# A decoder layer on one core: another order of the steps in the cross-attention loop

## What is computed

```python
x = _layernorm(x + _L0_attn_ref(x, W_K, W_Q, W_V, W_O))
# cross-attention; IMG_LEN = 257 > 256, so only the image half has tokens
q = rms_norm(linear(x, q_w, q_b), norm_q_w).reshape(B, L, NH, HD)      # NH 16, HD 16
k_img = rms_norm(linear(ctx_img, k_img_w, k_img_b), norm_k_img_w).reshape(B, -1, NH, HD)
v_img = linear(ctx_img, v_img_w, v_img_b).reshape(B, -1, NH, HD)
x = _layernorm(x + linear(attention(q, k_img, v_img), o_w, o_b))
x = _layernorm(x + _L0_ffn_ref(x, gate_w, gate_b, w1, b1, w2, b2))     # top 2 of 8 experts
```

## Time and profile before

| | us |
|---|---|
| median of 3 runs | 660.62 |
| lowest and highest | 660.0 and 664.72 |
| the profiled execution, whole | 664.72 |
| its span, first to last instruction | 663.0 |
| PE busy in the span | 559.1 |
| DVE, ACT, POOL busy | 364.5, 308.3, 166.1 |

### The profile page before, as it was taken

How to read it: one execution, slowest core, us unless ns; L and a number is a source line. 1 busy time by engine, 2 the same in 40 slices (tenths; PEclk the granted TensorE clock), 3 DMA queues, 4 the chain that set the end, 5 groups by cost and what they waited for, 6 DMA issues and landing times.

```text
span 663.0 us, 12586 instructions
## 1 busy us (share of the span) xinstructions
PE 559.1 (84%) x3867; PEld 482.7 (73%) x3867; DVE 364.5 (55%) x1134; ACT 308.3 (46%) x831; POOL 166.1 (25%) x267
## 2 busy tenths in 40 slices
PE   3899999999999999999686898783627999999940
PEld 2789898989989898988564555452416999999940
DVE  5175656565555656566755467621253655655645
ACT  1464545545554545445442565432123546446423
POOL 4131313131211122010368850105230000000153
PEclk9999999999999999999887799868567999999985
DMA  8640403123040405500000000001211442552324
GB/s 276 210 175 17 175 17 136 54 76 113 22 152 32 158 0 223 236 1 1 1 0 1 1 4 2 1 1 64 72 55 31 160 165 76 220 198 91 120 80 123
DMA packets 18403, 58.74 MB, mean 89 GB/s; under 512 B 3169, under 2 KB 7521, under 8 KB 13761
## 3 DMA queue, kind: packets, MB, share of 16 engines
q1 hardware_dynamic: 14048, 38.00, 16.0%
q10 hardware_dynamic: 1728, 12.58, 5.0%
q0 software_dynamic: 2592, 7.74, 3.4%
HBM read 35.83 MB, written 22.41 MB: 88 GB/s over the span
## 4 chain that ended last, share of the span: by engine, by line
PE 71%; DVE 8%; POOL 7%; issue 5%; ACT 3%; DMA 3%; DVEq 1%; POOLq 0%; SPq 0%; ACTq 0%
PE bank L549 12%; PE bank L551 11%; PE bank L550 11%; PE bank L927 6%; PE bank L606 4%; PE bank L588 4%; PE bank L596 3%; PE bank L763 3%; PE bank L779 3%; PE bank L607 2%; PE bank L587 2%; DVE w_lo L1516 2%; PE bank L707 2%; POOL x_slots L468 1%; PE bank L810 1%
## 5 line engine op out<-in xcount | busy, mean ns | idle before, releaser
L1151 ACT ACTIVATE hT<-bank,b 128x128 f32<-128x128 f32 x152 | 53.4, 368 | 57.6 <-PE bank L927 55.1
L927 PE MATMUL bank<-xgT,w 128*128 128x128 f32 x608 | 73.4, 280 | 1.2 <-DVE xgT L1509 0.7
L927 PEld LDWEIGHTS bank<-xgT,w 128*128 128x128 f32 x608 | 71.7, 196 | 1.8 <-issue 1.1
L1047 ACT ACTIVATE xPT<-bank 128x512 f32<-128x512 f32 x64 | 38.1, 599 | 61.8 <-PE bank L763 61.1
L1315 DVE TENSOR_REDUCE xnmax<-bank 128x2 f32<-128x512 f32 x64 | 43.8, 690 | 40.6 <-PE bank L742 39.9
L549 PE MATMUL bank<-xT_hi,wqk_hi 128*128 128x512 f32 x128 | 56.3, 440 | 11.0 <-DVE wqk_lo L1191 11.0
L1200 DVE CUSTOM_DVE_ANT_0 Sm<-bank,mask 128x128 f32<-128x128 f32 (+1 forms) x128 | 40.7, 356 | 33.7 <-PE bank L588 33.7
L967 ACT ACTIVATE Pr<-Sm,nmax 128x128 f32<-128x128 f32 x64 | 25.8, 403 | 70.5 <-DVE nmax L1200 70.4
L551 PE MATMUL bank<-xT_hi,wqk_lo 128*128 128x512 f32 x128 | 51.0, 399 | 0.0
L550 PE MATMUL bank<-xT_lo,wqk_hi 128*128 128x512 f32 x128 | 50.9, 398 | 0.0
L549 PE MATMUL bank<-w_hi,hT_hi 128*128 128x256 f32 x152 | 44.7, 294 | 3.9 <-DVE hT_lo L1537 3.9
(11 more groups left out here) (213 smaller groups left out, 1514.0 us busy)
## 6 DMA issues: line engine op xcount, KB each, us to landing
w<-in_w ACTq DMA_DIRECT2D x12, 1024.0 KB, 6.3
w_raw<-in_w_attn SPq DMA_DIRECT2D x32, 256.0 KB, 3.5
x_slots<-w SPq DMA_DIRECT2D x8, 1024.0 KB, 5.5
y_slots<-w SPq DMA_DIRECT2D x7, 1024.0 KB, 7.4
w<-in_w SPq DMA_DIRECT2D x4, 1024.0 KB, 7.8
xg<-x_slots SPq DMA_DIRECT2D x20, 128.0 KB
y_slots<-ys POOLq DMA_DIRECT2D x19, 128.0 KB, 2.0
xT_raw<-in_xT SPq DMA_DIRECT2D x2, 512.0 KB, 5.6
```

The lines of the kernel that those rows point to most:

```text
L927: last = mm(bank[f % 4][:, 0:P], w1e[:, c, f * P:(f + 1) * P], xgT[:, c, :], start=c == 0, stop=c == DC - 1)
L1047: A(xPT[j % 8][:, :, :], ps_xt[j % 2][:, :].rearrange("p (a n) -> p a n", a=2), ACT.Exp)\
L1151: A(hT[:, f, :], bank[f % 4][:, 0:P], ACT.Gelu_apprx_tanh, bias=b1[:, e, f:f + 1])\
```

## The change

All three lists of steps are rearranged; no operation is added or left out. PE now issues `x_scores(i)` first in a step, then `m_unit`, `q_unit`, `xo_unit`, `stack_half` and the gate's parts, and only then `x_scores_t(j)`, `x_pv`, `z_transposes` and `z_back`. The stack halves of a sequence stand in steps 6 to 9 and 11 to 14 of the sequence before, no longer in 0 to 13 with gaps. The query projections of tiles 4 to 7 stand two steps earlier. The output projections stand in pairs, at steps 37, 53 and 69. ACT copies the maxima before the exponentials and reads the stack before `z_evac` and `xz_evac`; DVE reads the stack before `z_normalise`.

```diff
-        STACK_AT = (0, 1, 3, 5, 7, 9, 11, 13)
-        XO_AT = (47, 48, 52, 53, 68, 69, 85, 86)
+        STACK_AT = (6, 7, 8, 9, 11, 12, 13, 14)
...
-        STEPS_X = XO_AT[-2]
+        STEPS_X = ITEMS + LAG + UNIT
...
-                pe.wait_ge(s["stk_evac_act"], stack_reads(8 * B - 1)[0])
-                pe.wait_ge(s["stk_evac_dve"], stack_reads(8 * B - 1)[1])
+                pe.wait_ge(s["stk_evac_act"], stack_reads(8 * min(b + 2, B - 1) + 7)[0])
+                pe.wait_ge(s["stk_evac_dve"], stack_reads(8 * min(b + 2, B - 1) + 7)[1])
...
-                if 0 <= j < ITEMS:
-                    x_scores_t(j)
                 if i < ITEMS:
                     x_scores(i)
                 if i >= UNIT and i % UNIT == 1 and i <= ITEMS + 1:
                     m_unit(i // UNIT - 1)
-                if j >= 13 and (j - 13) % UNIT == 0 and j - 13 < ITEMS:
-                    z_back((j - 13) // UNIT)
-                if j >= 5 and (j - 5) % GROUP == 0 and j - 5 < ITEMS:
-                    x_pv((j - 5) // GROUP)
-                if j >= 7 and (j - 7) % GROUP == 0 and j - 7 < ITEMS:
-                    z_transposes((j - 7) // GROUP)
-                if b == 0 and h in (2, 4, 6, 8):
-                    q_unit(3 + h // 2)
-                if i in XO_AT:
-                    xo_unit(XO_AT.index(i))
+                if b == 0 and h in (0, 2, 4, 6):
+                    q_unit(4 + h // 2)
+                if j >= 24 and (j - 24) % XH == 0:
+                    xo_unit(2 * ((j - 24) // XH))
+                    xo_unit(2 * ((j - 24) // XH) + 1)
                 if b + 1 < B and h in STACK_AT:
+                    if h == STACK_AT[0] and b >= 2:
+                        pe.wait_ge(s["xo_added"], 2 * (b - 1))
                     stack_half(8 * (b + 1) + STACK_AT.index(h))
...
+                if 0 <= j < ITEMS:
+                    x_scores_t(j)
+                if j >= 5 and (j - 5) % GROUP == 0 and j - 5 < ITEMS:
+                    x_pv((j - 5) // GROUP)
+                if j >= 7 and (j - 7) % GROUP == 0 and j - 7 < ITEMS:
+                    z_transposes((j - 7) // GROUP)
+                if j >= 13 and (j - 13) % UNIT == 0 and j - 13 < ITEMS:
+                    z_back((j - 13) // UNIT)
...
+                if i >= UNIT and i % UNIT == 1 and i <= ITEMS + 1:
+                    m_evac(i // UNIT - 1)
                 if 0 <= j < ITEMS:
                     x_exps(j)
-                if i >= UNIT and i % UNIT == 1 and i <= ITEMS + 1:
-                    m_evac(i // UNIT - 1)
+                if b == 0 and h in (1, 3, 5, 7):
+
+                    if h == 1:
+                        q_squares(2)
+                        q_squares(3)
+                    q_squares(4 + h // 2)
+                if b + 1 < B and h - 1 in STACK_AT:
+                    stack_read(8 * (b + 1) + STACK_AT.index(h - 1))
+                if i in (62, 63, 76):
+                    x2t_evac((62, 63, 76).index(i))
                 if j >= 6 and (j - 6) % GROUP == 0 and j - 6 < ITEMS:
                     z_evac((j - 6) // GROUP)
...
                 if i < ITEMS:
                     x_max(i)
+                if b == 0 and h in (1, 3, 5, 7):
+                    q_add(4 + h // 2)
+                if b + 1 < B and h - 1 in STACK_AT:
+                    stack_read(8 * (b + 1) + STACK_AT.index(h - 1))
                 if j >= 12 and (j - 12) % UNIT == 0 and j - 12 < ITEMS:
                     z_normalise((j - 12) // UNIT)
...
-                if i - 1 in XO_AT:
-                    xo_add(XO_AT.index(i - 1))
-                if i in (54, 70):
-                    dve.sem_inc(s["stats_ready"], 1)
+                if j >= 24 and (j - 24) % XH == 0:
+                    xo_add(2 * ((j - 24) // XH))
+                    xo_add(2 * ((j - 24) // XH) + 1)
+                    if j > 24:
+                        dve.sem_inc(s["stats_ready"], 1)
```

More of the change, by code:

```diff
@@ L1111, in _ @@
                     xz_evac((j - 14) // UNIT)
[L1112 to L1121, removed]
             norm_root(3, TT - 2, TT)
```

## The result

| | before | after |
|---|---|---|
| median, us | 660.31 (4 runs, 659.66 to 664.72) | 690.11 (4 runs, 684.86 to 701.87) |
| profiled execution, us | 664.72 | 684.74 |
| its span, us | 663.0 | 682.1 |
| mean granted clock of the span | 0.918 | 0.897 |
| first `x_scores` to first `x_slots` of POOL, us | 114.2 | 131.7 |

A forecast was written before the change was run, and what follows sets the result against it. PE's own instructions were taken to bound the cross-attention loop. Terms of +11.2, +3.2, +4.3, +1.4, -10.1 and 0 summed to +10.0 us, put on the median of 660.62 us: 670.6 us, range 657 to 678 us.

The forecast's parts named there:

- The clock: Assumption of the whole sum: the granted clock stays as it was, 1.2 GHz for much of the loop.
- the clock makes it worse: Rival: uneven PE work in the loop brings two or three more clock drops, +6 to +9 us; chance 0.12.
- Separated scores: Loop steps with something between the two scores, 26 of them, each cost another 0.43 us on PE: +11.2 us.
- Stack banks: Consecutive stack halves make PE wait for ACT's late read of the bank, 0.77 us at most each: +3.2 us.
- Borders: At three sequence borders the first x_scores waits 1.43 us for DVE's read of the last half: +4.3 us.
- Query projections: q_unit of steps 2, 4, 6 waits 0.73 us each for DVE to empty the one bank: +1.4 us.
- Waits that go: PE's loop waits of 5.2 and 2.2 us for POOL's stacks and 2.7 us for z_tok vanish: -10.1 us.
- Gate and tail: Steps 68 and 69 save 0.7 us, x_scores_t after x2t_unit(2) on the way to the gate adds 0.7: 0.
- Covered: Rival: lone scores hide beside waits or overlap what follows, half price and no stack bank waits, +1.2 us; chance 0.25.
- faster: Rival: the 5.2 us gap at POOL pulled the clock down; without it PE runs at 2.4 GHz, 656 us; chance 0.10.
- What would show it: Profile signs: L741 and L762 apart at 0.43 us each, ACT and border waits, first x_slots at about 463 us.

The follow-up runs named there:

- e7_twin: The changed kernel with x_scores_t also issued beside x_scores in the 26 separated steps, 52 matmuls later overwritten; 677.34 us, ratio 1.017 to the kernel before.
- e1: The changed kernel with x_scores_t put back directly behind x_scores, everything else as changed; 664.62 us, ratio 0.999 to the kernel before.
- e4: The changed kernel with ACT's stack read ahead of the exponentials and DVE's ahead of the maxima, scores still separated; 668.85 us, ratio 1.002 to before.
- e3: The changed kernel with extra unread 128-row matmuls in the light steps and at the sequence borders; 690.63 us, ratio 1.036 to the kernel before.

## Why the prediction was wrong

The sign was right, and every mechanism of the sum is in the trace. The time, 690.11 us, lies 12 us above the range. Without the clock the sum was too high: +10.0 us forecast, +4.1 measured as the rest. Point by point:

- **The clock, the step that failed.** "This takes the clock as it was." The sum puts a change of the clock at nothing. It was not as it was: 62.8 us of PE's work ran at 1.2 GHz, not 30.0, by the split +13.4 us of the loop's 17.5. e7_twin shows that this is a cause and not a mark: with nearly the same waits, and all useful work in the same order, the loop is 13.3 us shorter when the empty rows are filled. The rival "the clock makes it worse" named it with a chance of 0.12 and 6 to 9 us; it is what happened, and it cost 13. It also looked for the trigger in light parts and borders only. It had not thought of the lone matmuls, which e7_twin fills, nor that two small causes would meet in it (e1, e4).
- **Separated scores, forecast +11.2:** +8.8 by e1, 0.33 by the row. The `x_scores` half was priced right (0.42), `x_scores_t` at 0.34 was not, where the next `x_scores` follows it (where the products with V follow, from 389.56 to 389.99 us, it takes the full 0.43). The term counted a second 0.43 us for a step of which 0.76 us is the whole. The Trainium skill (TensorE: Matmul & The Clock Gate, "Back-to-back issue gap") would make this term an estimated 5.7 us. The measurement lies between the two, and with the clock's part the separation cost far more than either.
- **Stack banks, forecast +3.2:** +2.5. The wait of step 24 was forecast at 0.77 and is 0.99, for the cause given.
- **Borders, forecast +4.3:** three waits of 1.4 us each, 4.2, right in place, cause and size.
- **Query projections, forecast +1.4:** +3.2. Three waits of 1.2 where 0.73 was worked out. The 0.73 put two lone `x_scores`, of steps 1 and 2 for example, at 2 x 0.43 us. But neighbouring heads lie in different halves of the rows, and with no stack half between them the two run side by side, as a pair does; then 0.73 + 0.43 = 1.16 is due:

```profile
341.13 0.51 PE L741 MATMUL bank<-XK,QS 64*128 64x256 f32 x4
342.84 1.10 PE L729 MATMUL bank<-w_x,xT 128*128 128x256 f32 x4 [1.20 <-DVE q_tok L1309]
```

- **Waits that go, forecast -10.1:** -9.5, of which 0.6 is left at `stack_q`. The waits for `zt` and `xz`, left as they were, went from 7.5 to 7.9 in the loop.
- **Gate and tail, forecast 0:** 0.4 us behind the loop's end.
- The waits alone thus come to -0.5 us (19.4 to 18.9 idle), forecast -1.2. With +8.8 that is +8.3 and not the +4.1 measured as the rest, so some 4 us of PE's work are missing. Three times 0.43 us of them are the lone `x_scores` that now run side by side, which the waits for `q_tok` take back. What the others are stays open; the split by one ratio may hold part of them.
- **Covered and faster** are both out. A parted pair cost its 0.33 us, and no long gap was left, but the clock fell all the same. The faster rival's premise, that the 5.2 us gap pulled the clock down, is not borne out: after has no such gap, and runs at 1.2 GHz from 347.5 to 371.4 and from 409.0 to 436.3.
- **What would show it:** L741 and L762 apart, 0.42 and 0.34 and not 0.43 each; ACT's read 0.99; the borders 1.4 three times; no `stack_k` wait; the first `x_slots` at 471.37 and not 463. The last is the one that was wrong by much, and it is the clock.

What stays open is the exact trigger of each fall. Filling the rows (e7), filling the light steps (e3), taking 5 us of waits away (e4) and joining the pairs (e1) each bring much of the clock back: 0.87, 0.92, 0.84 and 0.90 in the loop, against 0.74. The runs show that fuller and steadier work on PE held it here, not which of these counts most.

## What to carry to other kernels

Two matmuls that use half of the rows each belong side by side in PE's stream; the order that parted them here cost twice, its own time and the clock. Before taking a stretch of PE at its old pace, read the granted clock beside PE's work for each stretch and price a fall as well; in a kernel that already runs partly at 1.2 GHz, "the clock as it was" may be the least safe line of a sum, as it was here. Reads that free a bank go ahead of work that nobody on the way to the end waits for.

## What the hardware showed unexpectedly

- More work, less time: 52 matmuls with no use, issued into empty rows, make the loop 13.3 us shorter and bring the ratio to before from 1.041 down to 1.017 (e7), with the granted clock of the loop at 0.87 instead of 0.74.
- The clock falls without a long gap. Ahead of 409.0 us PE's longest wait in 10 us was 0.99, and after it PE stayed at 1.2 GHz for 27.3 us while it was busy for 25.7 of them. The Trainium skill (TensorE: Matmul & The Clock Gate, "A second HAM failure mode: psum-queue depth-cycling") tells of a kernel whose frequent short idle times between groups of matmuls made the clock go up and down. The trace agrees in that only short waits stand ahead of this fall; but e7 keeps these waits (PE idle for 20.1 us in the loop, after 18.9) and holds the clock there, so they are not the whole of it.
- A 64-row matmul of 256 columns alone takes 0.17 to 0.21 us at the high clock, by the distance to the start of what follows (0.17 where the next `x_scores` follows in step 23, 0.21 where a stack half does), and 0.37 at the low one.
